# The softmax-free attention's reciprocals taken one head ahead, and the router's steps set singly between its sums

## The chip, the cores and the metric

The kernel runs on one core of a Trainium2 chip. The metric is the device time of one execution in microseconds (us); lower is better. One core has five engines that run side by side and meet at semaphores: PE (TensorE, matrix products), DVE (VectorE), ACT (ScalarE), POOL (GpSimd) and SP (SyncE), which here only issues transfers. Each engine carries out its own list of instructions in order: an instruction that waits for a semaphore holds up all that stand behind it on that engine, and nothing else.

## The reference, cut to what matters

Four batches of 512 positions with 128 features go through three layers with residuals. The change touches the second layer's last step and the third layer's routing, so only those are shown:

```python
# layer 2: 16 heads; qp is relu(features of q) + eps, kvs and ks_sum come from 77 context rows
num = jnp.einsum('blhm,bhmd->blhd', qp, kvs)
den = jnp.einsum('blhm,bhm->blh', qp, ks_sum)
att = num / den[..., None]
x = x + jnp.einsum('blhd,hdk->blk', att, Wo)
# layer 3: mixture of 8 experts, the best 2 for each position
xf = layernorm(x)
logits = xf @ router_w.T
top_w, top_i = lax.top_k(softmax(logits), 2)      # then made to sum to 1
g, u = xf @ w_gate[e].T, xf @ w_up[e].T           # for the two chosen experts e
x = x + sum over the two of weight * (silu(g) * u) @ w_down[e].T
```

## The kernel before

The whole of the first layer and the context's keys and values (the first 78 us) are not touched. What follows has two parts.

**Attention, 80 to 197 us.** Four batches n (0 to 3, `NB`) of 16 heads k (`H`) each; every head has four tiles t of 128 positions (`TPB`). The heads are numbered through as f = 16 n + k. Wo is already folded into the values, so a head's result is summed straight into the residual X. For one head:
- PE runs `features(n, k)`: three matrix products of 512 columns (L245 to L247) into `z_bank`.
- ACT makes `relu_z` from them (L666), then `q` (L583).
- PE runs `numerators` three heads later (`LAG`): in PE's step k stand features(k), then numerators(k - 3). They are four products of 130 columns (L1184), one for each tile; column 128 of each is the denominator. They write to `num`, which has four banks: two for even heads and two for odd ones. Tiles 0 and 1 share the head's first bank, tiles 2 and 3 its second. So ahead of tile 0 PE waits until DVE has done the sums of tiles 0 and 1 of the head two before, ahead of tile 2 until it has done those of tiles 2 and 3 (`att_done`, counted over all sums).
- DVE runs `weighted_sum`: one reciprocal of the four denominators (L918, waits for `num_done`, all four numerators of the head), then four sums X = num * rden + X (L922), one for each tile.

**The routing of batch m = n - 1 goes on beside the attention of batch n.** DVE: statistics and moments of the finished rows (L928, L931) ahead of head 0. POOL: their inverse root (L526, L531), `rstd`. DVE: `third_norm`, four scalings into `rows` (L936) behind head 0. PE: `turn_rows` transposes them (L1047) in its step 5. ACT copies them to y3T in its step 5 and fills the second copy of the rows there. PE: `router_logits` (L1196) in step 6. DVE: the best two and what follows (L954 to L970) in one run behind head 3. PE: `ranks` (L1203 to L1211) in step 8, which waits for `taken` (L966). DVE: places and weights (L974 to L988) in one run behind head 4. All these steps count up one semaphore `route`, 21 for each batch. POOL then sends the batch's 2 x 4 tiles of rows to `dispatched` by indirect DMA (L546, `scatter`), once all 21 are done. POOL has one list: batch m + 1's inverse root stands behind batch m's eight scatters. In batch 3, DVE also works out the experts' block table (L874 to L902), three steps behind each head from head 5 on.

**Experts, 195 to 262 us.** 39 blocks of 128 rows go through PE, ACT, DVE and POOL; SP loads each block's rows (`xb`, L377) and weights (L383). SP issues the first loads of `xb` when the scatters of batches 0 to 2 have landed, and those from block 16 on when batch 3's have. Batch 3's own routing stands beside blocks 2 to 5. At the end SP reads the results back and DVE adds them (L1038).

The order on every engine is written out by hand: the numbers `DVE_ROUTE`, `PE_Y3`, `ACT_Y3` and the like say behind which head a step stands.

Of the kernel before, what the change touches and what calls it, by code (L numbers as in the profile page):

```python
# [14 lines left out]
I32 = mybir.dt.int32  # L15
# [5 lines left out]
P = 128  # L21
NB = 4
# [35 lines left out]
def decoder_kernel(nc, x, ctxT, wuv, bu, bv, woaT, bo, coef, wk, wv, wq, wo, projT, router, wgu, wd,  # L58
                   out, xs, ys):
    with ExitStack() as ctx:  # L60
# [76 lines left out]
        rows = sb("rows", [P, TOPK, TPB, ROW])  # L137
# [11 lines left out]
        slot_i = sb("slot_i", [P, TPB, TOPK], I32)  # L149
# [71 lines left out]
        dest_done, sent = sem("dest_done"), sem("sent")  # L221
# [56 lines left out]
        TAKEN_STEP, DIFF_STEP = 11, 13  # L278
# [57 lines left out]
        def _(sp):  # L336
# [54 lines left out]
            sp.wait_ge(sent, 16 * TOPK * TPB * (NB - 1))  # L391
# [16 lines left out]
            sp.wait_ge(sent, 16 * TOPK * TPB * NB)  # L408
# [19 lines left out]
        def _(pool):  # L428
# [94 lines left out]
            def third_norm(m):  # L523
# [4 lines left out]
                if not isinstance(m, int) or m > 0:  # L528
                    wait_alone(pool, sent, m * 16 * TOPK * TPB)
                pool.wait_ge(ln3_step, m * 2 + 1)  # L530
                g.tensor_tensor(rstd[:, :], var_eps[:, :], p_mhalf[:, 0:TPB], ALU.pow).then_inc(ln3_step, 1)  # L531
                g.tensor_copy(rows[:, :, :, P].bitcast(I32),
# [5 lines left out]
            def scatter(m, t):  # L538
# [6 lines left out]
                for k in range(TOPK):  # L545
                    g.indirect_dma_start(  # L546
                        out=xs, out_offset=bass.IndirectOffsetOnAxis(ap=slot_i[:, t, k:k + 1], axis=0),
                        in_=rows[:, k, t, :], in_offset=None).then_inc(sent, 16)
# [25 lines left out]
        def _(act):  # L574
# [77 lines left out]
            def second_rows(m):  # L652

                act.wait_ge(y3_done, m * TPB + TPB)
                copy(rows[:, 1, :, 0:P], rows[:, 0, :, 0:P]).then_inc(y3_twice, 1)
# [5 lines left out]
            def attention(n, m):  # L661
                for k in range(H):
# [12 lines left out]
                    if m is not None and k == ACT_Y3:  # L675
                        turned_rows(m)
                        second_rows(m)
                    if m is not None and k == ACT_SECOND:
                        second_silu(m)
# [25 lines left out]
        def _(dve):  # L705
# [148 lines left out]
            def table_steps(first, count, start, stop):  # L854

                for make, wait in blocks_table(first, count)[start:stop]:
# [56 lines left out]
            def weighted_sum(n, h):  # L913

                f = n * H + h
                dve.wait_ge(num_done, f * TPB + TPB)
                banks = num[:, 2 * (h % 2):2 * (h % 2) + 2, 0:2 * HA].rearrange("p b (t c) -> p b t c", t=2)
                v.reciprocal(rden[:, h % 2, :].rearrange("p (b t) -> p b t", t=2), banks[:, :, :, P]).then_inc(rden_done, 1)  # L918
                wait_past(dve, att_done, f * TPB)
# [420 lines left out]
```

## Time and profile before

| what | value |
|---|---|
| median of 3 runs | 311.84 us (311.74 to 313.47) |
| span of the profiled execution, first to last instruction | 276.2 us |
| PE busy | 247.8 us, 90% |
| DVE busy | 190.4 us, 69% |
| ACT busy | 164.0 us, 59% |
| POOL busy | 124.3 us, 45% |
| granted clock of PE | 0.978 of full speed |

The span leaves out what lies ahead of the first and behind the last instruction; between it and the median lie 35.6 us. Busy shares are means over stages that differ. In the attention PE and DVE are both busy nearly all the time, so what a change there is worth is read from who waits for whom, head by head.

### The profile page before, as it was taken

How to read it: one execution, taken by the hardware profiler on the slowest of the kernel's cores; microseconds unless marked ns; L12 is line 12 of the kernel's file. 1: busy time of each engine (PE TensorE's matmuls, PEld its weight loads, DVE VectorE, ACT ScalarE, POOL GpSimd, SP SyncE). 2: the span in 40 equal slices, each digit the busy share in tenths (PEclk: the TensorE clock that was granted, in tenths of full speed). 3: DMA queues.
4: the chain of work that ended last, by engine and by line, in shares of the span. 5: the costliest groups of instructions: out<-in, count | busy, mean ns of one | idle time of the engine just before them, and what ended most of it. 6: DMA issues, size and time to landing. Idle time of an engine off the chain costs nothing.

```text
span 276.2 us, 5724 instructions
## 1 busy us (share of the span) xinstructions
PE 247.8 (90%) x1697; PEld 211.5 (77%) x1697; DVE 190.4 (69%) x713; ACT 164.0 (59%) x343; POOL 124.3 (45%) x183
## 2 busy tenths in 40 slices
PE   7899999999999999989998999988899979999600
PEld 4658676676888999879977997967789979999600
DVE  4777759589658988988898888999877312222115
ACT  3566466465577777677776677755365646656400
POOL 5648899841101000217220732064256777777710
PEclk9999999999999999999999999999999999999965
DMA  6999999960004000001000100014779399984157
GB/s 203 280 244 198 198 203 196 194 92 0 2 1 152 2 0 2 2 0 54 26 4 0 48 31 2 2 39 153 194 209 298 122 269 298 343 252 117 41 189 266
DMA packets 38445, 34.03 MB, mean 123 GB/s; under 512 B 3581, under 2 KB 31234, under 8 KB 38288
## 3 DMA queue, kind: packets, MB, share of 16 engines
q1 hardware_dynamic: 35312, 28.96, 44.0%
q0 software_dynamic: 2272, 4.24, 4.4%
q10 hardware_dynamic: 832, 0.49, 0.6%
q8 instruction: 14, 0.23, 0.4%
q14 instruction: 15, 0.12, 0.2%
HBM read 19.80 MB, written 14.32 MB: 124 GB/s over the span
## 4 chain that ended last, share of the span: by engine, by line
PE 59%; DVE 24%; DMA 6%; issue 4%; POOL 3%; SPq 2%; ACT 1%; DVEq 0%; POOLq 0%; ACTq 0%
DVE X L922 11%; PE num L1184 10%; PE bank L1269 10%; PE bank L1145 5%; PE num L1279 5%; PE num L1123 5%; PE num L245 3%; PE num L247 3%; PE bank L245 3%; PE num L246 3%; PE bank L1087 3%; PE bank L246 2%; PE bank L247 2%; DMA wo_sb<-in_wo 2%; DVE X L1038 2%
## 5 line engine op out<-in xcount | busy, mean ns | idle before, releaser
L922 DVE SCALAR_TENSOR_TENSOR X<-num,rden,X 128x128 f32<-128x128 f32 x256 | 72.1, 344 | 6.6
L1184 PEld LDWEIGHTS num<-kvw_sb,q 128*128 128x128 f32 x512 | 65.9, 190 | 12.1 <-ACT q L583 5.7
L1184 PE MATMUL num<-kvw_sb,q 128*128 128x130 f32 x512 | 68.7, 277 | 3.6 <-DVE X L922 3.6
L666 ACT ACTIVATE relu_z<-bank 128x512 f32<-128x512 f32 x64 | 38.2, 596 | 21.6 <-PE bank L247 21.5
L546 POOL DMA_INDIRECT dispatched<-rows,slot_i x32 | 31.3, 977 | 41.1 <-DVE rows L988 32.6
L566 POOL DMA_INDIRECT expert_out<-yo,xb x39 | 38.2, 978 | 14.1 <-issue 9.1
L583 ACT ACTIVATE q<-relu_z 128x512 f32<-128x512 f32 x64 | 40.4, 632 | 6.7 <-DVE acc L841 0.8
L1269 PE MATMUL bank<-xT,wgu_sb 128*128 128x128 f32 x312 | 41.5, 276 | 0.0
L1022 DVE TENSOR_TENSOR hid<-bank,silu_g 128x256 f32<-128x256 f32 x39 | 16.5, 423 | 35.5 <-ACT silu_g L691 35.1
L1269 PEld LDWEIGHTS bank<-xT,wgu_sb 128*128 128x128 f32 x312 | 38.0, 192 | 0.1
L245 PE MATMUL bank<-y2T_hi,feat_hi 128*128 128x512 f32 x64 | 30.4, 475 | 0.2
L691 ACT ACTIVATE silu_g<-bank 128x256 f32<-128x256 f32 x39 | 15.0, 384 | 19.6 <-PE bank L1269 18.7
L1279 PE MATMUL num<-wd_sb,hid 128*128 x156 | 24.5, 280 | 1.1 <-ACT yo L695 0.6
L247 PE MATMUL bank<-y2T_hi,feat_lo 128*128 128x512 f32 x64 | 25.1, 392 | 0.0
L246 PE MATMUL bank<-y2T_lo,feat_hi 128*128 128x512 f32 x64 | 25.1, 392 | 0.0
L526 POOL TENSOR_SCALAR var_eps<-moments_b 128x4 f32<-128x4 f32 x4 | 0.9, 229 | 46.9 <-DVE moments_b L931 46.9
L1279 PEld LDWEIGHTS num<-wd_sb,hid 128*128 128x128 f32 x156 | 20.4, 190 | 1.6 <-issue 1.5
L1123 PEld LDWEIGHTS num<-vw,kp 77*128 77x128 f32 x128 | 16.8, 190 | 3.2 <-issue 1.9
L792 DVE TENSOR_SCALAR kp<-num 77x512 f32<-77x512 f32 x16 | 10.9, 680 | 11.0 <-PE num L247 10.9
L583 ACT ACTIVATE vw<-num 77x512 f32<-77x512 f32 x16 | 9.5, 595 | 14.7 <-PE num L247 14.7
L695 ACT ACTIVATE yo<-num,xb 128x128 f32<-128x128 f32 x39 | 14.3, 368 | 4.7 <-PE num L1279 2.0
L1123 PE MATMUL num<-vw,kp 77*128 77x130 f32 x128 | 16.9, 274 | 0.0
(173 smaller groups left out, 402.5 us busy)
## 6 DMA issues: line engine op xcount, KB each, us to landing
wgu_sb<-in_wgu SPq DMA_DIRECT2D x39, 256.0 KB, 3.4
dispatched<-pad_row SPq DMA_DIRECT2D x3, 2795.0 KB, 32.7
xb<-dispatched SPq DMA_DIRECT2D x39, 65.0 KB, 3.5
y_back<-expert_out SPq DMA_DIRECT2D x4, 512.0 KB, 4.8
wd_sb<-in_wd SPq DMA_DIRECT2D x1, 1024.0 KB, 4.8
out<-X SPq DMA_DIRECT2D x4, 256.0 KB, 2.4
X<-in_x SPq DMA_DIRECT2D x3, 256.0 KB, 5.8
expert_out<-yo,xb POOLq DMA_INDIRECT x39, 4.0
```

The lines of the kernel that those rows point to most:

```text
L245: nc.tensor.matmul(ps, a_hi, b_hi, start=start, stop=False)
L246: nc.tensor.matmul(ps, a_hi, b_lo, start=False, stop=False)
L247: return nc.tensor.matmul(ps, a_lo, b_hi, start=False, stop=stop)
L546: g.indirect_dma_start(out=xs, out_offset=bass.IndirectOffsetOnAxis(ap=slot_i[:, t, k:k + 1], axis=0), in_=rows[:, k, t, :], in_offset=Non ...
L566: g.indirect_dma_start(out=ys, out_offset=bass.IndirectOffsetOnAxis(ap=xb[:, s % XRING, P:P + 1].bitcast(I32), axis=0), in_=yo[:, s % XRIN ...
L583: return a.activation(dst, src, ACT.Copy, **kw)
L666: a.activation(relu_z[:, k % 2, :], z_bank[k % 2], ACT.Relu).then_inc(relu_done, 1)
L922: v.scalar_tensor_tensor(tile_of(n, t), banks[:, t // 2, t % 2, 0:P], rden[:, h % 2, t:t + 1], tile_of(n, t), ALU.mult, ALU.add).then_inc( ...
L1123: last = nc.tensor.matmul(ks_bank[u % 2][:, HA * i:HA * (i + 1)], kp[:, (u // 2) % 2, M * h:M * (h + 1)], vw[:, (u // 2) % 2, h, :], start ...
L1184: nc.tensor.matmul(num[:, 2 * (h % 2) + t // 2, HA * (t % 2):HA * (t % 2 + 1)], q[:, h % 4, part], kvw_h, start=True, stop=True).then_inc( ...
L1269: last = nc.tensor.matmul(gu_bank[j % 2][:, part], wgu_sb[:, s % WRING, part], xT[:, j % 2, :], start=True, stop=True)
L1279: last = nc.tensor.matmul(dn_bank[j % 2][:, 0:P], hid[:, j % 2, part], one_expert(wd_sb[:, bass.ds(e, 1), part]), start=c == 0, stop=c == 1)
```

## The change

**Reciprocals one head ahead.** `weighted_sum` is called for each tile. The reciprocal of head f + 1 now stands between the second and the third sum of head f (`DVE_NEXT = 1`), with its wait for all four numerators of head f + 1. This holds for all 64 heads.

**Routing's steps singly, over eleven heads.** For batches n = 1 and 2 every routing step of DVE stands behind a single sum, from head 0 to head 10 (`beside_late`). PE's three steps move from 5, 6, 8 to 7, 8, 11, ACT's to 7, 9 (the second copy) and 11. For n = 3 PE and ACT keep their steps; DVE's are set behind single sums of heads 3 to 5 (`beside_last`), and the table's one by one behind each sum from the third of head 5.

**Rows and places twice.** `rows` and `slot_i` get two buffers, taken in turn, and `sent` becomes two semaphores, so that the scatters of one batch need not have landed before the next one's rows are written.

```diff
-        DVE_NORM = 0
-        DVE_ROUTE = (3, 3, 3, 3, 3, 4, 4, 4)
-        DVE_TABLE = 5
-        ACT_Y3 = 5
-        ACT_SECOND = 8
-        PE_Y3, PE_LOGITS, PE_RANKS = 5, 6, 8
+        DVE_NEXT = 1
+        ACT_Y3, ACT_TWICE, ACT_SECOND = (5, 7), (5, 9), (8, 11)
+        PE_Y3, PE_LOGITS, PE_RANKS = (5, 7), (6, 8), (8, 11)
+        DVE_TABLE = (5, 2)
...
-            def weighted_sum(n, h):
+            def denominators(f):
+
+                dve.wait_ge(num_done, f * TPB + TPB)
+                banks = num[:, 2 * (f % 2):2 * (f % 2) + 2, 0:2 * HA].rearrange("p b (t c) -> p b t c", t=2)
+                v.reciprocal(rden[:, f % 2, :].rearrange("p (b t) -> p b t", t=2), banks[:, :, :, P]).then_inc(rden_done, 1)
+
+            def weighted_sum(n, h, t):
...
+                if t == 0:
+                    if f == 0:
+                        denominators(0)
+                    dve.wait_ge(rden_done, f + 1)
+                wait_past(dve, att_done, (f - 1) * TPB + t + 1)
+                v.scalar_tensor_tensor(tile_of(n, t), banks[:, t // 2, t % 2, 0:P], rden[:, f % 2, t:t + 1], tile_of(n, t),
+                                       ALU.mult, ALU.add).then_inc(att_done, 1)
+                if t == DVE_NEXT and f + 1 < NB * H:
+                    denominators(f + 1)
...
+            def beside_late(m, k, t):
+
+                if k == 0:
+                    third_stats(m, t)
+                if k == 1 and t < 2:
+                    third_moments(m, 2 * t)
+                    third_moments(m, 2 * t + 1)
+                if k == 2:
+                    third_norm(m, t)
...
+            def beside_last(m, k, t):
+
+                if (k, t) == (0, TPB - 1):
+                    for i in range(TPB):
+                        third_norm(m, i)
+                if (k, t) == (3, 3):
+                    for i in range(TPB):
+                        top(m, i)
+                    for i in range(TPB):
+                        top_index(m, i)
+                    top_number(m)
+                if (k, t) == (4, 0):
+                    choose(m)
+                if (k, t) == (4, 1):
+                    take(m)
+                    difference(m)
...
+                        late = m < NB - 2
+                        if k == PE_Y3[late]:
                             turn_rows(m)
```

On DVE, the attention of batch 1, from its head 0 on. Before (X<-num,rden,X is a sum, rden<-num the reciprocal):

```order
L928 BN_STATS stats<-X 128x6 [waits att_done]
L928 BN_STATS stats<-X 128x6 x3
L931 BN_AGGR moments_b<-stats 128x2 [waits ln3_stats]
L931 BN_AGGR moments_b<-stats 128x2 x3
L918 RECIPROCAL rden<-num 128x4 [waits num_done]
L922 SCALAR_TENSOR_TENSOR X<-num,rden,X 128x128 [waits rden_done,att_done]
L922 SCALAR_TENSOR_TENSOR X<-num,rden,X 128x128 x3
L936 TENSOR_SCALAR rows<-X,moments_b,rstd 128x128 [waits ln3_step]
L936 TENSOR_SCALAR rows<-X,moments_b,rstd 128x128 x3
```

The same place of the changed kernel:

```order
L933 SCALAR_TENSOR_TENSOR X<-num,rden,X 128x128 [waits att_done,rden_done]
L940 BN_STATS stats<-X 128x6 [waits att_done]
L933 SCALAR_TENSOR_TENSOR X<-num,rden,X 128x128 [waits att_done]
L922 RECIPROCAL rden<-num 128x4 [waits num_done]
L940 BN_STATS stats<-X 128x6 [waits att_done]
L933 SCALAR_TENSOR_TENSOR X<-num,rden,X 128x128 [waits att_done]
L940 BN_STATS stats<-X 128x6 [waits att_done]
L933 SCALAR_TENSOR_TENSOR X<-num,rden,X 128x128 [waits att_done]
L940 BN_STATS stats<-X 128x6 [waits att_done]
```

The reciprocal has moved from ahead of the first sum to behind the second one of the head before, and two of the four statistics stand between it and the head's last sum.

On DVE, batch 3, from the sums of its head 3 to `taken`, on which PE's ranks wait. Before:

```order
L918 RECIPROCAL rden<-num 128x4 [waits num_done]
L922 SCALAR_TENSOR_TENSOR X<-num,rden,X 128x128 [waits rden_done,att_done]
L922 SCALAR_TENSOR_TENSOR X<-num,rden,X 128x128 x3
L954 MAX top_v<-bank 128x8 [waits logits_full]
L954 MAX top_v<-bank 128x8 x3
L958 MAX_INDEX top_i<-top_v,bank 128x8 [waits route]
L958 MAX_INDEX top_i<-top_v,bank 128x8 x3
L961 CAST top_f<-top_i 128x8 [waits route]
L962 TENSOR_TENSOR chosen<-top_f,iota_e 128x64 [waits route]
L966 TENSOR_TENSOR taken<-chosen 128x32 [waits route]
```

And now, from the reciprocal of head 4 behind the second sum of head 3:

```order
L922 RECIPROCAL rden<-num 128x4 [waits num_done]
L933 SCALAR_TENSOR_TENSOR X<-num,rden,X 128x128 [waits att_done] x2
L959 MAX top_v<-bank 128x8 [waits logits_full] x4
L963 MAX_INDEX top_i<-top_v,bank 128x8 [waits route] x4
L967 CAST top_f<-top_i 128x8 [waits route]
L933 SCALAR_TENSOR_TENSOR X<-num,rden,X 128x128 [waits att_done,rden_done]
L971 TENSOR_TENSOR chosen<-top_f,iota_e 128x64 [waits route]
L933 SCALAR_TENSOR_TENSOR X<-num,rden,X 128x128 [waits att_done]
L922 RECIPROCAL rden<-num 128x4 [waits num_done]
L976 TENSOR_TENSOR taken<-chosen 128x32 [waits route]
```

Two reciprocals, with their waits for the numerators of heads 4 and 5, now stand ahead of `taken`; before, only that of head 3 did.

## Rows read from the trace of the kernel before

**Rows 1.** Waits, of PE and of DVE: engine, line, releaser, total us, times, longest
```profile
PE num L1184 <- DVE X L922: 3.6, 9, 0.7
PE num L1261 <- DMA xb<-dispatched: 1.8, 2, 1.5
...
DVE rden L918 <- PE num L1184: 3.5, 21, 0.2
```
**Rows 2.** Timeline of PE, batch 0: start us, us, what, pieces
```profile
95.15 0.48 PE L245 MATMUL bank<-y2T_hi,feat_hi 128*128 128x512 f32 x1
...
95.93 1.05 PE L1184 MATMUL num<-kvw_sb,q 128*128 128x130 f32 x8
...
97.53 1.05 PE L1184 MATMUL num<-kvw_sb,q 128*128 128x130 f32 x8
```
**Rows 3.** Timeline of DVE, the same heads
```profile
95.44 0.18 DVE L918 RECIPROCAL rden<-num 128x4 f32<-128x4 f32 x1 [0.15 <-PE num L1184]
95.72 1.13 DVE L922 SCALAR_TENSOR_TENSOR X<-num,rden,X 128x128 f32<-128x128 f32 x4
```
**Rows 4.** Timeline, a head of batch 1 whose numerators waited for sums
```profile
122.29 1.13 DVE L922 SCALAR_TENSOR_TENSOR X<-num,rden,X 128x128 f32<-128x128 f32 x4
...
123.05 1.14 PE L1184 MATMUL num<-kvw_sb,q 128*128 128x130 f32 x8 [0.72 <-DVE X L922]
```
**Rows 5.** Timeline of PE, batch 1, head 0 to batch 2, head 0
```profile
108.59 1.05 PE L1184 MATMUL num<-kvw_sb,q 128*128 128x130 f32 x8
...
113.47 0.65 PE L1047 MATMUL bank<-ident,rows 128*128 128x128 f32 x4 [0.58 <-DVE rows L936]
...
115.55 0.95 PE L1196 MATMUL bank<-router_sb,y3T 128*128 128x8 f32 x8
...
119.61 0.18 PE L1203 MATMUL bank<-taken,before 128*128 128x32 bf16 x1
...
137.38 1.05 PE L1184 MATMUL num<-kvw_sb,q 128*128 128x130 f32 x8
```
**Rows 6.** Timeline of DVE, batch 1, steps of the routing
```profile
109.54 0.88 DVE L928 BATCH_NORM_STATS2 stats<-X 128x6 f32<-128x128 f32 x4
110.45 0.38 DVE L931 BATCH_NORM_AGGREGATE moments_b<-stats 128x2 f32<-128x6 f32 x4
...
112.30 1.12 DVE L936 TENSOR_SCALAR rows<-X,moments_b,rstd 128x128 f32<-128x128 f32 x4 [0.17 <-POOL rstd L531]
...
117.29 0.39 DVE L954 MAX8 top_v<-bank 128x8 f32<-128x8 f32 x4
...
119.18 0.17 DVE L970 TENSOR_SCALAR l_diff<-l_diff 128x4 f32<-128x4 f32 x1
119.26 0.18 DVE L918 RECIPROCAL rden<-num 128x4 f32<-128x4 f32 x1
```
**Rows 7.** Timeline of PE, batch 3, numerators of heads 0 and 4
```profile
166.25 1.05 PE L1184 MATMUL num<-kvw_sb,q 128*128 128x130 f32 x8
...
174.87 1.05 PE L1184 MATMUL num<-kvw_sb,q 128*128 128x130 f32 x8
```
**Rows 8.** Timeline of DVE, batch 3: last routing step, last head, first expert block
```profile
179.67 0.17 DVE L988 TENSOR_SCALAR rows<-rows 128x4 f32<-128x4 f32 x1
...
196.01 1.12 DVE L922 SCALAR_TENSOR_TENSOR X<-num,rden,X 128x128 f32<-128x128 f32 x4
...
198.38 0.39 DVE L1022 TENSOR_TENSOR hid<-bank,silu_g 128x256 f32<-128x256 f32 x1
```
**Rows 9.** Timeline of POOL, batch 2's last scatter
```profile
189.63 0.96 POOL L546 DMA_INDIRECT dispatched<-rows,slot_i  x1 [0.30 <-issue]
```
**Rows 10.** Timeline, first loads of expert rows, their first use, first gate
```profile
193.21 0.86 SPq L377 DMA_DIRECT2D xb<-dispatched  x2
...
195.13 0.78 PE L1261 MATMUL bank<-ident,xb 128*128 128x128 f32 x2
...
197.06 0.38 ACT L691 ACTIVATE silu_g<-bank 128x256 f32<-128x256 f32 x1 [0.83 <-PE bank L1269]
```

More of the change, by code:

```diff
@@ new lines, in _, with before_step, top, top_index @@
+            kk, ke, e3 = [P, TPB, TOPK], [P, TPB, TOPK, E], [P, TPB, E]
+            def before_step(m, step):
+                wait_alone(dve, route, m * ROUTE_STEPS + step + 1)
+            def top(m, t):
+                dve.wait_ge(logits_full, m + 1)
+                v.max(top_v[:, t, :], logits[:, t, :]).then_inc(route, 1)
+            def top_index(m, t):
+                before_step(m, TPB)
+                v.max_index(top_i[:, t, :], top_v[:, t, :], logits[:, t, :]).then_inc(route, 1)
@@ new lines, in top_number, with choose, take @@
+            def top_number(m):
+                before_step(m, 8)
+                v.tensor_copy(top_f[:, :, :], top_i[:, :, 0:TOPK]).then_inc(route, 1)
+            def choose(m):
+                before_step(m, 9)
+                v.tensor_tensor(chosen[:, :, :, :], over(top_f[:, :, :], 3, ke),
+                                iota_e[:, :].unsqueeze(1).unsqueeze(1).broadcast_to(ke), ALU.is_equal).then_inc(route, 1)
+            def take(m):
+                before_step(m, 10)
+                v.tensor_tensor(taken[:, :, :], chosen[:, :, 0, :], chosen[:, :, 1, :], ALU.add).then_inc(route, 1)
@@ new lines, in slots_chosen, with places, second_weight @@
+            def slots_chosen(m):
+                before_step(m, 15)
+                v.tensor_tensor(slot_k[:, :, :, :], chosen[:, :, :, :], over(slot_e[:, :, :], 2, ke), ALU.mult).then_inc(route, 1)
+            def places(m):
+                before_step(m, 16)
+                v.tensor_reduce(slot_f[:, :, :], slot_k[:, :, :, :], AX.X, ALU.add).then_inc(route, 1)
+            def second_weight(m):
+                dve.wait_ge(silu_w_done, m + 1)
+                v.tensor_tensor(rows[:, m % 2, 1, :, P + 1], l_silu[:, :], l_inv[:, :], ALU.mult).then_inc(route, 1)
@@ L990, in routing @@
-                return [top, top_index, choose, take, difference, slots, places, weights]
-            def attention(n, m):
-                if m is not None:
-                    third_moments(m)
-                    steps = list(zip(DVE_ROUTE, routing(m), strict=True))
+                        third_moments(m, t)
                 for k in range(H):
@@ L1189, in turn_rows @@
                 pe.wait_ge(y3_done, m * TPB + TPB)
-                transposes(t_bank, [rows[:, 0, t, 0:P] for t in range(TPB)]).then_inc(tb_full, 1)
+                transposes(t_bank, [rows[:, m % 2, 0, t, 0:P] for t in range(TPB)]).then_inc(tb_full, 1)
             def router_logits(m):
```

220 lines of the change are left out of this document (130 added, 90 removed).

## The prediction, made before the changed kernel ran

> **What bounds the kernel now.** Read first the waits of PE and DVE [rows 1]. PE waits little: 3.6 us for sums (9 times) and 1.8 us for expert rows. DVE waits for numerators only 21 times in 64 heads. So in the attention the two take turns as the bound, and what counts is the head loop.
>
> The timeline gives PE's head [rows 2]: numerators start every 1.58 to 1.60 us (95.93, 97.53; 1.585 is the mean of many), 0.78 of it the features in front of them (95.15 to 95.93), 0.80 the numerators. The numerators are reported done 1.05 after their start and DVE's reciprocal starts 0.04 later, 1.09 after [rows 2, 3]. Reciprocal to first sum is 0.28, and four sums cost 0.26 each: a DVE that is behind takes 1.32 a head, against PE's 1.585.
>
> When PE is behind DVE [rows 4], the second sum starts at 122.29 + 0.26 = 122.55 and the numerators at 123.05, 0.50 later, and they are 0.09 longer (1.14 for 1.05): a sum's start reaches PE's timetable after 0.58.
>
> Batch 1 takes 137.38 - 108.59 = 28.79, which is 3.45 over 16 bare heads [rows 5]. Of it about 1.6 is PE's own work (transposes 0.4, logits 0.9, ranks 0.3, the stretches of PE's list that these rows start), the rest waiting: 0.8 for the normed rows, 0.8 for sums [rows 4, 5].
>
> Then the end of the attention, by two chains. Batch 2's last routing step ends at 179.84 [rows 8]; eight scatters follow, the last ends at 190.59 [rows 9], SP's first load is issued at 193.21 and PE uses it at 195.13 [rows 10]. So routing's end to first block is 15.3 us. The other chain is DVE's: last sum at 196.01 + 3 x 0.26 = 196.79, the first block's `hid` at 198.38, 1.6 later [rows 8], although its gate was ready at 197.44 [rows 10]. Both chains must move for the experts to start earlier; either moves them later.
>
> **The change part by part.** I count from the start of a numerator group and add rows.
>
> *The reciprocal ahead.* It hides its own 0.28, replaced by its issue cost. The trace has no reciprocal followed by a sum that doesn't need it. The nearest is a small step followed by an independent one, 119.18 to 119.26, 0.08 [rows 6]; the upper bound is its whole duration, 0.18 [rows 3]. I take 0.08. But the reciprocal of head f + 1 waits for all numerators of f + 1, and sums 3 and 4 of head f now stand behind it, on which PE's numerators of head f + 2 wait from tile 2 on. The loop is: reciprocal 0.08, third sum 0.26, fourth sum to PE 0.58, the second half of the numerators to the next reciprocal 1.09 - 0.44 = 0.65 (0.44 for the first two tiles, half of the 0.8 and what starts them). Sum: 1.57 us. PE's head is 1.585: a bare head still costs nothing, but with 0.015 of slack in place of 0.26. DVE can't catch up any more, and every step set between the reciprocal and the fourth sum is added to PE's head.
>
> *Batch 0.* The norm of batch 3 of layer 2 stands behind head 0 as before; the sums behind it are late for numerators in one or two heads: +0.4.
>
> *Batches 1 and 2.* Between reciprocal and fourth sum now stand: head 0, two statistics of 0.22 (0.88 / 4) [rows 6]: 0.42 beyond slack; head 1, two moments: 0.14; head 2, four scalings of 0.26 [rows 6], all within one round of the loop and so all paid, 1.14 with the head before's arrears; heads 5 to 9, pairs of `max`, two index steps, and single small steps of 0.08 to 0.14: 0.15 + 0.35 + 0.26. Sum 2.5 of waits. PE's own 1.6 stays, and the waits for normed rows and for sums (1.8) go, since PE's steps are later. So 4.1 over bare heads in place of 3.45: +0.6 for each, +1.2 for both.
>
> *Batch 3 up to its last routing step*, from the start of numerators of head 0 (166.25 before [rows 7]). Numerators 0 are done at 1.09; reciprocal; sums 3 and 4 of the head before at 1.17 and 1.43. Before, these had been done a head earlier; the statistics wait for them: 1.81, moments end 3.02 (0.88 and 0.38 [rows 6]). Sums at 3.02, 3.28, reciprocal, sums at 3.62, 3.88. POOL needs from last moment (2.95) to scaling 1.6 (110.45 + 0.23 to 112.30 [rows 6]), so 4.6. But batch 2's scatters now start late (behind head 10): 10.75 us from routing's end to the last scatter's end [rows 8, 9]. Routing's end stands 7.1 before this batch's start, so POOL is free at 3.6 to 3.9 in place of 3.1: +0.5. Scalings at 5.1, the last at 5.9; transposes 0.39 later, 6.3 (1.5 of PE waiting since numerators 2). Then features 6 and numerators 3, logits, features 7: numerators 4 start at 10.0. Before it was 174.87 - 166.25 = 8.62 [rows 7].
>
> Numerators 4 done at 11.1, reciprocal, sums 3 and 4 of head 3, then `max` 0.42, indices 0.8, number: before it took 119.18 - 117.29 = 1.9 for all up to L970 [rows 6]. Sum, `chosen`, sum, reciprocal 5, `taken`: PE can start ranks at 13.8. It is through numerators 5 at 12.4, so it waits 1.4. Numerators 6 then are done at 16.0, and only behind their reciprocal come the last two steps: routing ends at 16.3. Before: 179.84 - 166.25 = 13.6. So +2.7, and with the batches before 0.4 + 1.2 + 2.7 = **+4.3 at the scatters**. The first gate is ready at 197.44 + 4.3 = 201.75.
>
> *Batch 3 to its end.* Head 6's numerators start at 14.9; six heads of 1.585 and 1.1 of table steps within the loop give head 12's at 25.5, done 26.6. Three rounds of the loop, 4.7, then sums 3 and 4 and four more: last sum at 32.7. Before 196.79 - 166.25 = 30.5. So +2.1, and 0.4 + 1.2 + 2.1 = +3.7 at DVE: `hid` at 202.1. Later than 201.75, so this chain counts: **+3.7**.
>
> *Experts.* Same work. The dependent steps of batch 3's own routing are reordered so that two of them no longer wait for another; about 0.2 off the wait for block 16's rows (1.5 [rows 1]) : -0.2. The second buffer of rows frees a wait that was already over by then: 0.
>
> Sum: 276.2 + 3.5 = 279.7 for the span. The 35.6 between span and median is untouched, so 311.84 + 3.5 = **315.3 us**.
>
> [...] Row: an independent small step starts 0.08 after one that takes 0.17 [rows 6]. [...]
>
> **Rivals.**
> - *DVE's throughput decides, faster.* If the fourth sum reaches PE in less than 0.58 and DVE stays a head behind, the wait for f + 1's numerators is already over when the reciprocal comes up. Then each head saves 0.28 - 0.08 = 0.2 of DVE in the 26 us where it is behind in batch 3 (16 heads, 3.2), dependent steps save some 0.1 each, and the 0.8 waits in batches 1 to 3 (rows and sums) shrink. Limited by the scatter chain, I give -2.5: 309.3. For it: DVE waited for PE in only 21 of 64 heads [rows 1]. Against it: at 1.57 the loop lets no backlog last. It decides if the loop is under about 1.45.
> - *A wash.* The stalls in batches 1 and 2 hide in the 3.45 that they replace, and ranks in batch 3 wait less than 1.4: 0 to +1.5, 312.5.
> - *The loop is over PE's head.* With 0.18 for the reciprocal it is 1.67; each bare head then pays 0.09, some 45 of them 4 us, on top of 3.5: 319.5. It decides from a loop of 1.60 on.
>
> **How the numbers follow.** Forecast 0.62, faster rival 0.12, wash 0.18, loop over PE's head 0.08. The forecast's own range: 0.08 less for each sum to reach PE gives +2, a reciprocal of 0.11 gives +5.5: 313.8 to 317.3. The whole range, with most of the wash and part of both outer rivals, is 311.0 to 319.0. A change of 1% (3.1 us) is about what a measurement can tell. Slower by more than that (over 314.96) holds 0.46 of the forecast's 0.62 and the last rival: 0.54. Within 1%: the rest of the forecast and nearly all the wash, 0.33. Faster: 0.13.
>
> **What would show it.** Right: PE's waits for sums rise from 3.6 to some 9 us, spread over many small ones at heads 0 to 2 and 5 to 9; bare heads stay at 1.585, DVE's reciprocals wait in nearly every bare head; ranks of batch 3 wait 1.4; batch 2's last routing step ends at 184.1 and the first expert block is at 199.4. Wrong: bare heads over 1.60 (third rival); the last step before 179.8 (faster); batches 1 and 2 under 28.8 us (wash).

## The result, and the profile after

| | median | range |
|---|---|---|
| before, 5 runs | 311.74 us | 310.62 to 313.47 |
| after, 5 runs | 318.85 us | 315.86 to 322.18 |

The ratio is 1.0231, with a 95% interval of 1.0175 to 1.0286: +7.1 us, slower, inside the predicted range and twice the forecast's +3.5. Four more comparisons, told below, put the change at about 1.01, so both numbers have to be explained.

On some chips both kernels take about 280 us, on others about 310; the trace of the kernel before from which the prediction was made (span 276.2) is of the first sort, while the runs of this first comparison are all of the second. I call the first sort *undisturbed*.

The profile of the changed kernel in the first comparison; the busy time of each engine, the granted clock in 40 slices (tenths of full speed), and the waits (engine, line, releaser, total us, times, longest):

```profile
PE 263.6 (82%) x1697; PEld 224.5 (70%) x1697; DVE 181.7 (57%) x713; ACT 162.4 (51%) x343; POOL 124.2 (39%) x183
...
PEclk9799999999999999997999899979995699979975
```
```profile
DVE rden L922 <- PE num L1298: 26.0, 40, 2.5
...
PE num L1394 <- DVE hid L1121: 14.5, 8, 6.0
PE num L1298 <- DVE X L933: 14.0, 10, 3.8
```

Its span is 320.4. The waits for sums have risen from 3.6 [rows 1] to 14.0 in only ten places. That isn't the many small waits that I had forecast. The same kernel on an undisturbed chip (e2_after_again, span 278.8) has this:

```profile
DVE rden L922 <- PE num L1298: 20.1, 43, 1.3
...
PE num L1376 <- DMA xb<-dispatched: 2.2, 2, 1.9
...
PE num L1298 <- DVE X L933: 2.1, 7, 0.4
...
PE bank L1317 <- DVE taken L976: 1.6, 2, 1.2
...
PE bank L1161 <- DVE rows L948: 1.4, 1, 1.4
```

Here the waits for sums have even gone down (3.6 to 2.1), and two others have become long: 1.6 for `taken` (the ranks), which was 0.4 before, and 1.4 in one piece for the normed rows, which was 1.9 in three. Another 3.4 of waiting for sums, in part the same time, is booked to PE's weight loads, where the trace before has none. DVE waits for numerators at 43 reciprocals, where it waited at 21 [rows 1]. This trace is what the prediction's steps can be held against; what the other trace adds is a section of its own.

### The profile page after: what moved, and what is told of

The parts are those of the page before. It is cut to its first block, busy times and chain, and to the rows that moved or that the text cites. A ratio compares the mean times of both kernels' runs of the same rounds, so it can differ in the third digit from the quotient of the medians.

```text
span 320.4 us, 5721 instructions
## 1 busy us (share of the span) xinstructions
PE 263.6 (82%) x1697; PEld 224.5 (70%) x1697; DVE 181.7 (57%) x713; ACT 162.4 (51%) x343; POOL 124.2 (39%) x183
## 4 chain that ended last, share of the span: by engine, by line
PE 70%; DVE 10%; another core or an unknown queue 7%; DMA 4%; issue 3%; ACT 2%; POOL 1%; SPq 1%; POOLq 0%; ACTq 0%
PE num L1298 17%; PE bank L1384 10%; PE num L1394 6%; PE bank L1259 5%; PE bank L246 4%; PE num L1237 4%; DVE X L933 4%; PE bank L248 4%; PE bank L247 4%; PE num L246 2%; PE num L248 2%; PE num L247 2%; PE bank L1201 2%; DMA wo_sb<-in_wo 2%
## 5 line engine op out<-in xcount | busy, mean ns | idle before, releaser
L1298 PEld LDWEIGHTS num<-kvw_sb,q 128*128 128x128 f32 x512 | 71.4, 198 | 25.3 <-DVE X L933 16.8
L1298 PE MATMUL num<-kvw_sb,q 128*128 128x130 f32 x512 | 75.3, 288 | 15.6 <-DVE X L933 14.0
L933 DVE SCALAR_TENSOR_TENSOR X<-num,rden,X 128x128 f32<-128x128 f32 x256 | 74.8, 336 | 0.0
L666 ACT ACTIVATE relu_z<-bank 128x512 f32<-128x512 f32 x64 | 38.1, 595 | 37.7 <-PE bank L248 27.6
L1384 PE MATMUL bank<-xT,wgu_sb 128*128 128x128 f32 x312 | 45.2, 292 | 3.3 <-issue 2.8
L1384 PEld LDWEIGHTS bank<-xT,wgu_sb 128*128 128x128 f32 x312 | 41.4, 207 | 4.2 <-issue 4.2
L1394 PE MATMUL num<-wd_sb,hid 128*128 x156 | 26.6, 296 | 14.7 <-DVE hid L1121 14.5
L1394 PEld LDWEIGHTS num<-wd_sb,hid 128*128 128x128 f32 x156 | 22.0, 203 | 16.5 <-issue 16.5
L922 DVE RECIPROCAL rden<-num 128x4 f32<-128x4 f32 x64 | 11.5, 180 | 38.3 <-PE num L1298 26.0
L246 PE MATMUL bank<-y2T_hi,feat_hi 128*128 128x512 f32 x64 | 31.4, 490 | 0.2
L248 PE MATMUL bank<-y2T_hi,feat_lo 128*128 128x512 f32 x64 | 26.2, 410 | 0.0
```

Of the source, the lines that this page charges most:

```text
L246: nc.tensor.matmul(ps, a_hi, b_hi, start=start, stop=False)
L248: return nc.tensor.matmul(ps, a_lo, b_hi, start=False, stop=stop)
L666: a.activation(relu_z[:, k % 2, :], z_bank[k % 2], ACT.Relu).then_inc(relu_done, 1)
L933: v.scalar_tensor_tensor(tile_of(n, t), banks[:, t // 2, t % 2, 0:P], rden[:, f % 2, t:t + 1], tile_of(n, t), ALU.mult, ALU.add).then_inc( ...
L1298: nc.tensor.matmul(num[:, 2 * (h % 2) + t // 2, HA * (t % 2):HA * (t % 2 + 1)], q[:, h % 4, part], kvw_h, start=True, stop=True).then_inc( ...
L1384: last = nc.tensor.matmul(gu_bank[j % 2][:, part], wgu_sb[:, s % WRING, part], xT[:, j % 2, :], start=True, stop=True)
```

## The experiments

### The change again, three more times, and the kernel before against itself

> The kernel before, profiled once more, so that two traces of like executions can be compared. The trace of before spans 276.2 us and its median is 311.8, while the changed kernel's trace spans 320.4 us at 322.2: the one has no pauses, the other has pauses of 1 to 6 us of PE in the four stretches in which POOL scatters rows. Theory L (the loop reciprocal, sums 3 and 4, numerators): the change costs by its longer waits, pauses are a property of the executions and both kernels have them alike; then a trace of before at about 310 us has pauses of some 34 us in all, in the same stretches (scatters and expert blocks). Theory S (the change brings the pauses in): such a trace has none, its span is near 276 and the 35 us lie outside it.

> The changed kernel unchanged, beside the others on one chip. Both theories: 1.0175 to 1.0286 of before, 317 to 320 us. Its trace shows whether the pauses of PE (142, 147, 175, 181, 203, 209, 240 and 248 us in the first trace) come back at the same instructions (then a mechanism of the kernel) or elsewhere (then of the execution).

> The changed kernel again, to have its ratio on whatever chip this job gets. The first comparison gave 1.0231 (1.0175 to 1.0286) where before took 311.7 us, the second 1.0106 (1.0064 to 1.0147) where before took 280.3. Theory C (the extra is of the chip, whose executions are interrupted by pauses of PE): where before takes about 280 the ratio is 1.008 to 1.015 again; where it takes 310 it is above 1.017. Theory N (noise of the first comparison): 1.01 to 1.02 on any chip.

> The changed kernel once more, beside those with its parts undone, for a chip of the slower sort. Theory C: ratio above 1.017 where before takes about 310 us, with half-clock stretches of PE inside the attention; 1.008 to 1.015 where it takes 280.

| kernel | this | before, same chip | ratio |
|---|---|---|---|
| before again (e1) | 279.92 | 280.27 | 0.9992 (0.9953 to 1.0031) |
| after (e2) | 283.09 | 280.27 | 1.0106 (1.0064 to 1.0147) |
| after (e8) | 283.2 | 280.31 | 1.0097 (1.0069 to 1.0125) |
| after (e12) | 283.28 | 280.42 | 1.0107 (1.0059 to 1.0156) |

On three undisturbed chips the change costs 2.8 to 2.9 us. The expectation for e2, 317 to 320 us, missed, since that chip turned out to be of the other sort. Where these arise, in us, counted in each trace from the first numerators (82.36 before, 83.31 in e2):

| stage | before | e1 (before) | after e2 | e8 | e12 |
|---|---|---|---|---|---|
| batch 0 | 26.23 | 26.21 | 26.34 | 26.32 | 26.35 |
| batch 1 | 28.79 | 28.75 | 28.95 | 28.95 | 28.94 |
| batch 2 | 28.87 | 28.84 | 28.95 | 28.97 | 28.98 |
| batch 3 to the last routing step | 13.59 | 13.57 | 16.21 | 16.26 | 16.25 |
| last sum's start | 114.44 | 114.33 | 116.16 | 116.18 | 116.21 |
| first `hid` | 116.02 | 115.90 | 117.73 | 117.76 | 117.79 |

The attention repeats to 0.1 us, so single traces can be compared there. Nearly all of what the attention loses arises in batch 3 before its last routing step (+2.6); by the last sum, which the experts' first `hid` follows, +1.7 of it is left. The medians say 2.8 to 2.9, so some 1.1 us more is lost in the experts, and no run places it: from the first `hid` to the end, the traces take 77.8 and 78.5 before and 77.8, 77.9 and 80.3 after, and e2's and e8's are the fastest executions of theirs.

In that part of batch 3, PE (e2), from numerators 0 at 167.56 to the ranks:

```profile
171.29 1.21 PE L1298 MATMUL num<-kvw_sb,q 128*128 128x130 f32 x8 [0.40 <-DVE X L933]
...
173.88 0.66 PE L1161 MATMUL bank<-ident,rows 128*128 128x128 f32 x4 [1.37 <-DVE rows L948]
...
181.38 0.19 PE L1317 MATMUL bank<-taken,before 128*128 128x32 bf16 x1 [1.20 <-DVE taken L976]
```

and DVE, from the scalings over the two reciprocals ahead of `taken` to the last two steps of batch 2's routing, behind yet another reciprocal:

```profile
172.70 1.12 DVE L948 TENSOR_SCALAR rows<-X,moments_b,rstd 128x128 f32<-128x128 f32 x4 [0.97 <-POOL rstd L531]
...
178.63 0.18 DVE L922 RECIPROCAL rden<-num 128x4 f32<-128x4 f32 x1 [1.28 <-PE num L1298]
...
181.08 0.17 DVE L922 RECIPROCAL rden<-num 128x4 f32<-128x4 f32 x1
181.17 0.16 DVE L976 TENSOR_TENSOR taken<-chosen 128x32 bf16<-128x32 f32 x1
...
183.47 0.18 DVE L922 RECIPROCAL rden<-num 128x4 f32<-128x4 f32 x1 [0.27 <-PE num L1298]
183.57 0.14 DVE L1010 TENSOR_SCALAR rows<-rows 128x4 f32<-128x4 f32 x1
183.62 0.16 DVE L1014 CAST slot_i<-slot_f 128x8 int32<-128x8 f32 x1
```

Of the two reciprocals ahead of `taken` only the first costs: DVE stands 1.28 for head 4's numerators, with the whole choice of the experts behind it. Head 5's, at 181.08, waits for nothing any more.

### Each part by itself

The reciprocals ahead alone: the kernel before with

```diff
+                    if t == 1 and f + 1 < NB * H:
+                        denominators(f + 1)
```

in `weighted_sum`, where each head's own reciprocal is gone but that of head 0, and no other part of the change. The steps alone (with the two buffers): the changed kernel with each head's own reciprocal,

```diff
-                    if f == 0:
-                        denominators(0)
+                    denominators(f)
...
-                if t == DVE_NEXT and f + 1 < NB * H:
-                    denominators(f + 1)
```

> The kernel before with one edit: the reciprocal of head f + 1 stands between the second and third sum of head f. All routing steps stay where they were, one buffer of rows. Theory L: bare heads stay at 1.58 to 1.60 us, every block of steps now stands behind sums that wait for the next head's numerators, so batch 2's routing ends later: slower by 2 to 5 us than before (1.006 to 1.016). Theory T (DVE's throughput counts): 0.2 us a head are saved where DVE is behind: faster by 2 to 4 us.

> The changed kernel with one edit undone: each head's reciprocal stands ahead of its own first sum again; steps stay single and late, rows and places double. Theory L: the loop is gone (1.32 us a head where DVE is behind), single steps wait less for one another, so batches 1 and 2 take 27.5 to 28.5 us and the whole is 0 to 3 us faster than before. Rival R (the late steps of batches 1 and 2, with their scatters up to the next batch's root, are the cost): slower than before by 2 to 5 us, as the changed kernel.

And the same two kernels on a chip of the other sort:

> The kernel before with the reciprocals ahead alone (1.026 where before takes 280 us). L1: 1.03 to 1.04 where before takes about 310 us, since the same change on top of the rest gave more there. L2: 1.020 to 1.026, the same microseconds or fewer. Where before takes 280 us: 1.024 to 1.029 again.

> The changed kernel with own reciprocals, steps single and late. L1 (the loop costs on the slower chips too): 0.985 to 0.995 on any chip. L2 (later steps and scatters cost there): 1.005 to 1.015 where before takes about 310 us, 0.990 where it takes 280.

| kernel | undisturbed | other sort |
|---|---|---|
| reciprocals ahead alone | 287.0, 1.0262 (1.0184 to 1.0341) | 319.59, 1.0354 (1.0277 to 1.0431) |
| steps singly alone | 277.7, 0.9896 (0.9785 to 1.0007) | 306.83, 0.9934 (0.9892 to 0.9976) |

On the other sort both came out as theory L1 had it, 1.03 to 1.04 and 0.985 to 0.995.

The change is the sum of a loss and a gain: +6.7 and -2.6 against the same before. The loss is clear, and more than the 1.006 to 1.016 that was expected of it; the gain's interval reaches 1.0007 here and is clear only on the other sort. Together they would be +4.1, and are +2.8. By stage, reciprocals ahead: batches 1 and 2 take 30.77 and 30.83 (+2.0 each), batch 3's first part 15.78 (+2.2). Steps alone: 27.73 and 27.75 (-1.1 each), 14.03 (+0.4). Three rows of the waits of the reciprocals alone show the price of a block of steps that stands between two reciprocals:

```profile
PE num L1192 <- DVE X L928: 3.6, 8, 0.6
PE bank L1211 <- DVE taken L974: 3.0, 4, 0.9
...
PE bank L1055 <- DVE rows L944: 2.6, 3, 0.9
```

Waits for `taken` in all four routings, where the kernel before has one of 0.4, and 2.6 for the normed rows, where it has 1.9. So the early reciprocal is the part that costs, in blocks or in single steps, and the single steps are worth more where it is early: batch 1 goes from 30.77 to 28.95, against 28.79 to 27.73 with own reciprocals. The wash and faster rivals fall with that: the early reciprocal saves nothing that shows.

### Where the reciprocal stands

One number of the changed kernel:

```diff
-        DVE_NEXT = 1
+        DVE_NEXT = 0
```

(behind the first sum, e5), or 3 (behind the fourth, e6 and e13); or each head's own in batch 3 only (e7):

```diff
-                    if f == 0:
-                        denominators(0)
+                    if f == 0 or n == NB - 1:
+                        denominators(f)
...
-                if t == DVE_NEXT and f + 1 < NB * H:
+                if t == DVE_NEXT and f + 1 < (NB - 1) * H:
```

> The changed kernel with DVE_NEXT = 0: the next head's reciprocal stands one sum earlier, behind the first sum, so three sums instead of two stand behind its wait. Theory L: the loop grows by one sum, 0.08 + 3 x 0.26 less the first + 0.58 + 0.65, from 1.57 to 1.83 us; that is over PE's bare head of 1.585, so bare heads in batch 0 take 1.83 us and the whole about 10 to 14 us more than the changed kernel (1.04 to 1.06 of before). Theory T (DVE's throughput): DVE's work is the same, so is the time.

> The changed kernel with DVE_NEXT = 3: the next head's reciprocal stands behind the fourth sum, no sum behind its wait, single steps may hide its latency. Theory L: the loop is gone, the time is that of the kernel with own reciprocals (0.985 to 0.995 of before). If hiding the reciprocal's 0.2 us a head were worth anything, it is under 0.985.

> The changed kernel, but in batch 3 (heads 48 to 63) each reciprocal stands ahead of its own head's first sum; batches 0 to 2 keep it one head ahead. The prediction put 2.7 of the scatters' 4.3 us of delay into batch 3, and the trace of the changed kernel on this chip shows 2.65 there and 0.3 in batches 1 and 2. Theory L: nearly all of the 5.4 us between the changed kernel and that with own reciprocals is in batch 3: 0.99 to 0.995 of before. If the reciprocals cost evenly over the heads: 1.005 of before.

> The changed kernel with the reciprocal behind the fourth sum. On a 280 us chip 0.990 as before. On a 310 us chip: if what costs there is the reciprocal's loop (theory L1), it is 0.99 there too and the changed kernel about 1.02; if what costs there is that steps and scatters lie later (theory L2), it is 1.005 to 1.015, like its earlier version (1.0126 there).

| kernel | this | ratio | batch 1 | batch 3, first part |
|---|---|---|---|---|
| behind the first sum (e5) | 294.03 | 1.0476 (1.0426 to 1.0527) | 32.58 | 16.85 |
| behind the second, the change (e8) | 283.2 | 1.0097 (1.0069 to 1.0125) | 28.95 | 16.26 |
| own in batch 3 (e7) | 280.6 | 0.9996 (0.9968 to 1.0025) | 28.95 | 14.46 |
| behind the fourth (e6) | 278.05 | 0.9904 (0.9863 to 0.9946) | 27.59 | 14.71 |

e13, the same kernel as e6, came to 279.71 (275.91 to 280.91; without an interval), beside 280.42 of before: by itself that is no difference. Its attention is e6's (27.59, 27.60 and 14.72). Behind two waits for expert rows of 1.1 to 1.3 us each the granted clock falls to 0.50 (1.2 GHz), until 200 in e6 and 203 in e13, from about 196 on; in the undisturbed traces of the kernel before and of the change it stays at 1.00 there.

With own reciprocals in batch 3 alone the change costs nothing (280.6 for 280.31). But e7's expectation, that nearly all of the 5.4 us between the change and own reciprocals everywhere lies in batch 3, missed: 2.6 do (283.2 to 280.6). The early reciprocal costs in batches 1 and 2 as well (28.95 for e4's 27.73); there the single steps' gain hides it.

e5 measures the loop. Its bare heads, on PE and on DVE:

```profile
94.74 1.14 PE L1298 MATMUL num<-kvw_sb,q 128*128 128x130 f32 x8
96.49 1.14 PE L1298 MATMUL num<-kvw_sb,q 128*128 128x130 f32 x8
```
```profile
95.92 0.18 DVE L922 RECIPROCAL rden<-num 128x4 f32<-128x4 f32 x1 [0.55 <-PE num L1298]
96.02 1.10 DVE L933 SCALAR_TENSOR_TENSOR X<-num,rden,X 128x128 f32<-128x128 f32 x4
97.66 0.18 DVE L922 RECIPROCAL rden<-num 128x4 f32<-128x4 f32 x1 [0.55 <-PE num L1298]
```

A head takes 1.75, of the loop and no longer of PE: from the reciprocal 0.10 to the next sum (96.02), 0.47 to the numerators that this sum frees (96.49), 1.17 to the next reciprocal (97.66). By the prediction's terms it would be 1.57 and one more sum, 1.83; it is 0.08 shorter. The changed kernel's own loop shows bare in the last heads of batch 3, where PE has no more features to compute. DVE (e2):

```profile
195.13 0.18 DVE L922 RECIPROCAL rden<-num 128x4 f32<-128x4 f32 x1 [0.29 <-PE num L1298]
...
196.62 0.18 DVE L922 RECIPROCAL rden<-num 128x4 f32<-128x4 f32 x1 [0.29 <-PE num L1298]
...
198.10 0.18 DVE L922 RECIPROCAL rden<-num 128x4 f32<-128x4 f32 x1 [0.29 <-PE num L1298]
```

That is 1.48 to 1.49 a turn, in e8 and e12 too. The single terms in the changed kernel, at a head of batch 1 that the steps hold up (e2), PE and DVE:

```profile
117.75 0.71 PE L1298 MATMUL num<-kvw_sb,q 128*128 128x130 f32 x4 [0.32 <-DVE X L933]
```
```profile
117.35 0.34 DVE L933 SCALAR_TENSOR_TENSOR X<-num,rden,X 128x128 f32<-128x128 f32 x1
...
118.50 0.18 DVE L922 RECIPROCAL rden<-num 128x4 f32<-128x4 f32 x1
118.60 1.10 DVE L933 SCALAR_TENSOR_TENSOR X<-num,rden,X 128x128 f32<-128x128 f32 x4
```

The fourth sum starts at 117.35, its numerators at 117.75 (0.40), the reciprocal at 118.50 (0.75), the next sum at 118.60 (0.10), and one sum more is 0.26: 1.51. In the last heads the sum is 0.24, which gives the 1.49.

### PE's steps one place earlier

With the reciprocal behind the fourth sum, PE's transposes, logits and ranks of batches 1 and 2 one head earlier, and DVE's steps to match:

```diff
...
-        PE_Y3, PE_LOGITS, PE_RANKS = (5, 7), (6, 8), (8, 11)
+        PE_Y3, PE_LOGITS, PE_RANKS = (5, 6), (6, 7), (8, 10)
...
```

> DVE_NEXT = 3 as in the kernel with the reciprocal behind the fourth sum, and the late routing of batches 1 and 2 one to one and a half heads earlier: transposes, logits and ranks in PE's steps 6, 7 and 10 in place of 7, 8 and 11, DVE's last step behind the third sum of head 8 in place of the first of head 10. Theory L with the scatters' knock-on: POOL is then free before batch 3's moments, so DVE no longer waits 1.3 us for the root, and PE no longer 1.5 us for the rows but 0.7: 0.5 to 1.5 us faster than that kernel, 0.985 to 0.989 of before. If the late scatters cost nothing: 0.990, the same.

> The kernel with the reciprocal behind the fourth sum and routing one to one and a half heads earlier, so far only run where before took 308.6 us (1.0126). On a 280 us chip: 0.985 to 0.989, since POOL is free before batch 3's moments. On a 310 us chip: 1.00 to 1.015 as before.

A miss both times. On a chip of the other sort e9 took 311.33, 1.0126 (1.0042 to 1.021); undisturbed, e14 took 283.09 (278.53 to 284.12, without an interval) against 280.42, a spread in which a difference of 1% can't be seen. The attention in e14's trace shows why there is no gain:

```profile
PE bank L1167 <- DVE rows L948: 4.4, 3, 1.7
```

PE comes to turn the normed rows before DVE has them, and waits 4.4 in three places (e6: 1.5 in one); batches 1 and 2 take 29.15 in place of e6's 27.6, and only batch 3's first part is shorter, 14.16 for 14.71. The change's later place for PE's steps is the right one.

### The two buffers, and the scatters moved

The two buffers for `rows` and `slot_i` alone, on the kernel before (e10), and with the scatters of batches 0 and 1 issued behind the next batch's root (e11, e15), in place of at their heads:

```diff
+                    if m and k == POOL_NORM:
+                        for t in range(TPB):
+                            scatter(m - 1, t)
...
-                        if m is not None and k == SCATTER[t]:
+                        if m == NB - 2 and k == SCATTER[t]:
```

> The kernel before with the two buffers of rows and places alone, and the two semaphores for the scatters. The prediction put this part at 0: 1.000 of before (0.997 to 1.003), and the same waits in the trace. If writing rows had waited for the scatters, it would be faster by 0.3 us or more.

> The kernel before with two buffers, and the scatters of batches 0 and 1 put behind the inverse root of the batch after: they run 15 to 20 us later, beside heads 1 to 8 of the next batch, in place of beside heads 6 to 13. On a chip where before takes about 280 us: 1.00 of before (0.995 to 1.005). On a chip where it takes 305 to 312: Theory P1 (PE pauses go with the scatters): the pauses that stood at 132 to 137 and 161 to 168 us in the trace of the kernel with two buffers alone move with them, to about 147 to 155 and 175 to 183. Theory P2 (pauses come at a pace of their own, or at a point of PE's list): they stay at 132 to 137 and 161 to 168.

> As the kernel with later scatters before (1.0026 where before takes 280.4 us), for a chip of the slower sort: P1, PE's pauses of 132 to 137 and 161 to 168 us move to about 147 to 155 and 175 to 183 with the scatters; P2, they stay.

> The changed kernel, as the measure beside the two that follow. Where before takes about 310 us: above 1.017, with half-clock stretches within the attention. Where it takes 280: 1.008 to 1.015, the third time.

e10: 309.86 for 308.57, 1.0049 (1.0012 to 1.0087), on the other sort of chip. That is 1.3 us slower, above the 1.003 that was expected and with its whole interval above 1: small, but not the nothing that it was priced at. The buffers alone did not run on an undisturbed chip. e11: 281.73 for 280.42, 1.0026 (0.999 to 1.0061), undisturbed. e15: 311.91 for 309.18, 1.0117 (1.0065 to 1.017), and e16, the change itself on that same chip: 312.75, 1.0117 (1.0042 to 1.0191), +3.6. The expectation that the change costs over 1.017 wherever before takes 310 us missed with that.

## What the slower chips add: pauses of PE beside the scatters

In each of the seven traces of that sort PE's work stops for 1 to 4.5 us at a time beside POOL's bursts of eight indirect scatters, and DVE and ACT wait for it. In the attention these stops begin 5 to 12 us after a burst's first scatter; some fall just behind its last. Two scatters of batch 0 in e10, the first and the last of eight, with PE and DVE at the same time:

```profile
124.76 1.25 POOL L548 DMA_INDIRECT dispatched<-rows,slot_i  x1 [10.62 <-DVE rows L990]
...
133.90 0.96 POOL L548 DMA_INDIRECT dispatched<-rows,slot_i  x1 [0.30 <-issue]
```
```profile
131.19 1.05 PE L1186 MATMUL num<-kvw_sb,q 128*128 128x130 f32 x8
```
```profile
133.38 0.18 DVE L920 RECIPROCAL rden<-num 128x4 f32<-128x4 f32 x1 [2.86 <-PE num L1186]
...
136.35 0.18 DVE L920 RECIPROCAL rden<-num 128x4 f32<-128x4 f32 x1 [1.56 <-PE num L1186]
```

The numerators of 131.19 are recorded as done at 132.24; the reciprocal that they release starts at 133.38, having waited 2.86, and ACT, which waits for the features behind them, starts at 133.43. (Ends of matrix products are modelled in these records, so whether PE stood still or only its signals came late can't be told.) PE then shows a "wait for DVE" of 1.48, which is only the pause coming back: DVE had waited for PE first. In e15 the eight scatters run from 141.58 to 151.67 instead, and so do the pauses move: up to 147.73 the heads are whole, and then

```profile
149.45 0.95 POOL L548 DMA_INDIRECT dispatched<-rows,slot_i  x1 [0.30 <-issue]
150.71 0.96 POOL L548 DMA_INDIRECT dispatched<-rows,slot_i  x1 [0.30 <-issue]
```
```profile
147.73 1.05 PE L1189 MATMUL num<-kvw_sb,q 128*128 128x130 f32 x8
```
```profile
150.24 0.18 DVE L923 RECIPROCAL rden<-num 128x4 f32<-128x4 f32 x1 [1.85 <-PE num L1189]
```

What follows is a stretch at half the clock. The columns are start and end, length, busy us (pieces) of PE, PE's weight loads, DVE, ACT and POOL, then the granted clock (1.00 is 2.4 GHz), DMA share, GB/s:

```profile
150.00:152.00 2.00, 0.72 (x6) 0.75 (x7) 1.31 (x5) 0.00 (x0) 1.37 (x2) 1.00 0.10 33
152.00:154.00 2.00, 0.70 (x5) 0.51 (x4) 0.60 (x4) 0.84 (x2) 0.00 (x0) 0.69 0.10 33
154.00:156.00 2.00, 1.54 (x4) 0.75 (x5) 1.70 (x11) 1.91 (x5) 0.00 (x0) 0.50 0.00 0
156.00:158.00 2.00, 2.00 (x9) 2.00 (x10) 1.47 (x7) 0.80 (x2) 0.00 (x0) 0.50 0.00 0
```

PE was busy for 1.4 of the 4 us ahead of 154, in whose second half the granted clock falls (0.69 on average); then it runs at 0.50, that is 1.2 GHz, although it is busy all of 156 to 158. In the first comparison's trace the same two signs stand in the stretches of its scatters, on PE and on DVE:

```profile
180.61 0.71 PE L1298 MATMUL num<-kvw_sb,q 128*128 128x130 f32 x4 [3.18 <-DVE X L933]
```
```profile
146.19 0.18 DVE L922 RECIPROCAL rden<-num 128x4 f32<-128x4 f32 x1 [3.22 <-remote]
...
179.88 0.18 DVE L922 RECIPROCAL rden<-num 128x4 f32<-128x4 f32 x1 [3.85 <-remote]
```

What a trace of this sort has over an undisturbed one of the same kernel, from the first numerators to the last sum: +10.0 for the two buffers (against the kernel before), +15.7 for the scatters moved, +17.1 for the change (both traces of it), +13.8 for the steps alone, +17.3 for the reciprocals alone. These are single executions, and the executions of a kernel there spread by 3 to 6 us. The experts are longer as well: 92.9 to 99.9 from the first `hid` to the end, where undisturbed traces take 77.8 to 81.3; there PE's longest gap, up to 8.5 us (e17), stands in or just behind batch 3's burst, and undisturbed traces have 1.2 to 2.7 there, a wait for block 16's rows. That pauses go with the scatters is shown by e10 and e15, and by e17 on e15's chip: scatters from 130.8 to 140.8, stops at 139.2 to 143.5. Why they arise, and why only on some chips, is not. The kernel before itself has no trace from such a chip; e10 differs from it by the two buffers.

## Why the prediction was right or wrong

**Batch 3 up to its last routing step: right, row by row.** Counted from numerators 0 (167.56 in e2):

| step | predicted | e2 |
|---|---|---|
| POOL free of scatters | 3.6 to 3.9 | 3.6 |
| scalings start | 5.1 | 5.14 |
| transposes | 6.3 | 6.32 |
| numerators 4 | 10.0 | 9.98 |
| ranks | 13.8 | 13.82 |
| routing ends | 16.3 | 16.22 |

The waits in it were forecast as 1.5 for rows and 1.4 for ranks, and are 1.37 and 1.20: the mechanism was right, and not only the number. e7, whose batch 3 is without early reciprocals, gives 14.46. This step carries the forecast's sign.

**The loop: right in kind, one term too long.** "Fourth sum to PE 0.58" and 0.65 from there to the reciprocal, 1.23 together, measure 0.40 and 0.75, 1.15 together; the reciprocal costs 0.10 for 0.08. The loop is 1.49 to 1.51, not 1.57, and PE's bare head 1.59. So the slack is 0.08 to 0.10 and not 0.015, and bare heads stay at PE's pace (95.32, 96.91, 98.50 in e2: 1.59). The row for 0.58 [rows 4] shows another wait than the loop's: there PE waits ahead of a head's first tile, 0.49 from the sum's start in all nine such waits of that trace (its 0.50 and 0.09 also make 0.59, not 0.58). The loop closes over the third tile, for which the kernel before never waited, and there it is 0.38 to 0.40 in all six of e2.

**Batches 0 to 2: +0.4 + 1.2 forecast, +0.35 measured.** The term that failed is "Sum 2.5 of waits". From the starts of numerators in batch 1 of e2 the heads over their bare length come to 1.9: 0.3, 0.45 and 0.7 ahead of the numerators of heads 3, 4 and 5, 0.3 ahead of those behind the ranks, 0.15 later. With 1.59 x 16 = 25.44 and PE's own 1.6 that makes 28.94. With a slack of 0.08 to 0.10 a round, arrears can be worked off between the steps, which fits this; no run tests it by itself. Of the +1.6 forecast here only a fifth came, and with it went the sign that was to show the forecast right: waits for sums are 2.1, not some 9.

**DVE's chain: +3.7 forecast, +1.7 measured** (last sum 114.44 to 116.16; `hid` 116.02 to 117.73). Of the 2.0 too much it inherits 1.25 from the batches before; 0.7 is batch 3's own: forecast +2.1, measured 31.92 - 30.55 = +1.4. The scatters' chain is +3.0 at routing's end for +4.3 forecast, and +2.1 at the first block (112.77 to 114.87; from routing's end to the first block it is 14.4 here, where the prediction kept before's 15.3). That both chains move by about the same was right; the forecast had both too long by 1.3 to 2.

**Experts: -0.2 forecast, about +1.1 measured** (2.8 to 2.9 less the 1.7 above), unplaced. That the undisturbed +2.8 comes near the forecast's +3.5 is therefore luck in part: 2.0 too much ahead of the experts, and 1.3 too little in them.

**"The 35.6 between span and median is untouched": wrong, the step that failed in the first comparison.** The prediction took it for time outside the span. In every run that lists both, time and span lie only 1.7 to 2.2 us apart (322.18 and 320.4 for the trace after). The 35.6 were therefore some 34 us *inside* the executions that the 311.84 stand for: a kind of execution that the trace read was not, with pauses and half-clock stretches. The prediction gave no reason for "untouched". By elimination the missing 3.6 of the 7.1 us lie in this term, since the rest of the sum was too large rather than too small: by the prediction's own rows the undisturbed change is +3.5, and on undisturbed chips it is +2.8 to +2.9. On the other sort it was +7.1 once and +3.6 once (e16), so the term does not always move, and what moved it in the first comparison isn't shown.

**What stays open.** Why the first comparison shows 1.0231 when four repeats on four other chips give 1.0106, 1.0097, 1.0107 and 1.0117. The traces say where to look: that of the first comparison and e16's take the same from the first numerators to the first `hid`, 134.97 and 134.85, and differ in the experts, 99.9 against 92.9 us, of which the change touches only batch 3's own routing steps. These are two single executions, and the first is the slowest of its five. Nor does the loop itself cost clearly more on the slower chips: the reciprocals alone are +10.4 for +6.7, with intervals that overlap, but the change over own reciprocals is 5.9 (e16, e17) for 5.4 (e2, e4). The share of chance in where the pauses fall wasn't measured.

**The rivals.** *Faster*: its condition, a loop under 1.45, was nearer than I thought (1.49), but early reciprocals saved nothing even so: without them the kernel is faster than the change on both sorts of chip (e4, e17). *A wash*: half right, its first part came true (stalls in batches 1 and 2 hide), its second not (ranks wait 1.2). *Loop over PE's head*: no, bare heads are 1.59; e5 is what it would look like. It was priced with a reciprocal that costs its full 0.18. The Trainium skill, "VectorE: DVE Perf Modes", section "The DRAIN you can't avoid", says that the next operation does not start until the pipeline is empty, but also that a next operation that is not held starts earlier. These records agree with the second: an independent sum starts 0.10 behind the reciprocal's start (96.41 to 96.51 in e2), while one that needs it starts 0.20 to 0.28 behind (e4 and the kernel before).

## A version that beats both

The single steps and the later places of PE's steps, with each head's own reciprocal (e4, e17: 0.9896 and 0.9934, the second with its whole interval below 1) or with the next one behind the fourth sum (e6: 0.9904, clear as well; its repeat e13 is 0.7 us under before, without an interval). They gain 2.3 to 2.6 us on before by the medians. In the attention batches 1 and 2 are 1.05 to 1.25 shorter each.

## What to carry to other kernels

A wait that is hoisted in an in-order queue, here a reciprocal that needs all of the next head's numerators, also holds back what stands behind it: count the loop that it closes (0.10 + 0.26 + 0.40 + 0.75 here) and compare it with the other engine's period, for each place where it could stand. Take each term from a wait of the same kind: ahead of the first tile it was 0.49, ahead of the third 0.40. Every step set inside that loop is paid from the slack, and here blocks of steps cost more than single ones (+6.7 against +2.8). And before a span is used as the base of a sum, hold it against the runs' times: a difference of 35 us is not overhead until a run that lists both says so.

## What the runs showed of the chip that I had not expected

Beside POOL's bursts of indirect scatters PE's work stops, for 1 to 4.5 us at a time in the attention, on some chips and not on others, and the granted clock often falls to 0.50 behind them (in 154 to 158 of e15); moving the scatters moved the stops. With that an execution is some 27 to 42 us longer (span 306.8 in e10 for 279.4 in e1, 320.4 in the first comparison's trace for 278.8 in e2), more than half of it in the experts in e10 and the first comparison. Behind two waits for expert rows of 1.1 to 1.3 us each the clock was at 0.50 too, from about 196 to 200 in e6 and to 203 in e13, on undisturbed chips. Of the 3.6 us by which e4's first `hid` comes earlier than before's, 2.6 are left in its median.
